# An adjacency kernel of two graph layers: 48 instead of 36 second-layer batches run during the read, and each chunk's work is spread over three slots

## What is computed

```
# layer 0
o  = (adj == 1) @ (x @ w1) + (adj == 2) @ (x @ w2) + (adj == 3) @ (x @ w3) + bias
x1 = layernorm(x + o)
# layer 1: attention over the neighbours
h  = x1 @ W.T + b
e  = leaky_relu(h @ we1 + be1 + (h @ we2 + be2).T, 0.01)
out = layernorm(x1 + softmax(where(adj > 0, e, -9e15), axis=1) @ h)
```

## Time and profile before

| | |
|---|---|
| median of 3 runs | 1693.44 us (1690.89 to 1693.66) |
| the profiled execution | 1693.23 us, its span 1691.6 us |
| TensorE (PE) matmuls busy | 1462.5 us, 86% of the span |
| VectorE (DVE) busy | 1094.2 us, 65% |
| ScalarE (ACT) busy | 959.4 us, 57% |
| GpSimd (POOL) busy | 202.4 us, 12% |
| mean granted TensorE clock | 0.951 of full speed |

### The profile page before, as it was taken

The page is one execution under the profiler, slowest core; times in us unless marked ns, Lnnn a source line. Parts: engine busy times, 40 slices in busy tenths (PEclk is TensorE's granted clock), DMA queues, the critical chain, the costliest instruction groups (busy, mean ns, idle before and its releaser), DMA issues. The chain is left out here.

```text
span 1691.6 us, 19291 instructions
## 1 busy us (share of the span) xinstructions
PE 1462.5 (86%) x6934; PEld 672.6 (40%) x6934; DVE 1094.2 (65%) x2384; ACT 959.4 (57%) x1454; POOL 202.4 (12%) x188
## 2 busy tenths in 40 slices
PE   3687686986998998989979489999999999999996
PEld 1333342442443443444434134444444444444443
DVE  3557666867697676667764766556666666666563
ACT  2233423624355444444633667777787878888774
POOL 1112214122122121120210400000000000000000
PEclk9889899997999998999989689999999999999998
DMA  9999889889888898897890210000011000000100
GB/s 118 122 129 103 97 86 109 97 76 105 87 91 94 79 97 95 77 110 82 84 112 4 62 38 7 25 25 2 26 44 32 25 26 26 26 26 25 32 1 14
DMA packets 122435, 106.45 MB, mean 63 GB/s; under 512 B 4768, under 2 KB 114912, under 8 KB 122336
## 3 DMA queue, kind: packets, MB, share of 16 engines
q0 software_dynamic: 67584, 67.12, 43.9%
q1 hardware_dynamic: 54752, 38.05, 7.9%
HBM read 294.39 MB, written 12.09 MB: 181 GB/s over the span
## 5 line engine op out<-in xcount | busy, mean ns | idle before, releaser
L968 ACT ACTIVATE neg_masks<-e_row,cols 128x512 int8<-128x512 f32 x1024 | 640.7, 708 | 208.4 <-PE ps L1164 149.4
L1164 PE MATMUL ps<-pos_masks,tables 128*128 128x512 fp8e4 x2048 | 622.3, 386 | 63.4 <-DVE pos_masks L597 58.3
L1164 PE MATMUL ps<-neg_masks,tables 128*128 128x512 fp8e4 x2048 | 619.4, 384 | 0.0
L1118 PE MATMUL ps<-edge_masks,tables 128*128 128x512 fp8e4 (+1 forms) x2048 | 479.3, 395 | 49.2 <-DVE edge_masks L576 34.1
L595 DVE TENSOR_TENSOR neg_masks<-pos_masks,neg_masks 128x2048 uint16<-128x2048 uint16 x128 | 161.7, 1263 | 281.9 <-ACT neg_masks L968 280.8
L1118 PEld LDWEIGHTS ps<-edge_masks,tables 128*128 128x128 f16 x2048 | 204.8, 101 | 308.5 <-DVE edge_masks L576 37.8
L1164 PEld LDWEIGHTS ps<-pos_masks,tables 128*128 128x128 f16 x2048 | 196.0, 99 | 319.1 <-issue 107.5
L1164 PEld LDWEIGHTS ps<-neg_masks,tables 128*128 128x128 f16 x2048 | 202.7, 99 | 251.4 <-issue 16.6
L576 DVE TENSOR_SCALAR edge_masks<-edges 128x512 uint16<-128x512 uint16 x512 | 109.2, 286 | 171.4 <-ACT edges L959 171.1
L953 ACT ACTIVATE packed_bf<-packed 128x1024 bf16<-128x1024 uint8 x64 | 67.4, 1053 | 211.3 <-DVE packed L566 211.3
L959 ACT ACTIVATE edges<-ps 128x1024 uint8<-128x1024 bf16 x64 | 65.5, 1023 | 190.2 <-PE ps L1130 190.2
(11 more groups left out here) (116 smaller groups left out, 642.7 us busy)
## 6 DMA issues: line engine op xcount, KB each, us to landing
adj_in<-adj POOLq DMA_DIRECT2D x128, 512.0 KB, 11.9
e_row<-e_scratch SPq DMA_DIRECT2D x30, 256.0 KB, 4.3
edges<-x SPq DMA_DIRECT2D x8, 512.0 KB, 12.6
x_rows<-x SPq DMA_DIRECT2D x8, 512.0 KB, 5.0
x_scratch<-x SPq DMA_DIRECT2D x8, 512.0 KB, 8.0
edge_masks<-x_scratch SPq DMA_DIRECT2D x16, 256.0 KB, 3.2
out<-adj_in SPq DMA_DIRECT2D x16, 256.0 KB, 2.5
part_scratch<-a_c_rows SPq DMA_DIRECT2D x14, 256.0 KB, 5.1
```

Source lines behind the costliest of these rows:

```text
L968: ins = e.activation(GN[:, n:n + GR].bitcast(I8), e1row[:, q % 2, :], ACT.Sign, bias=t2[:, JC * c + j:JC * c + j + 1])
L1118: ins = e.matmul(ps[:, h, :], v_hl[:, i, JC * c + j, :], U0[:, n:n + GR].bitcast(kind), start=c == 0 and j == 0 and i == 0, stop=c == NCH ...
L1164: ins = e.matmul(z_bank(q, k), tab[:, c, 2 * k + i, j, :], mask[:, n:n + GR].bitcast(F8A), start=first and j == 0 and i == 0, stop=final a ...
```

## The change

It alters the plan, the order of work in a slot on all five engines, and which engine does three steps.

- **Plan.** 48 batches have slots during the read: 2, 6, 8, 8, 8, 8, 8 behind the groups 0 to 6. From slot 29 on each slot has one. Halves 0 and 1 are worked on in four segments, 2 to 13 in two. 34 segments instead of 30; 18 of them add a stored partial sum instead of 14. Of the 80 remaining batches, the halves 6 to 13 have four each. They start in slot 69.
- **Layer 0 two slots behind.** `layer0(k-2)` instead of `layer0(k-1)` in slot k. `edge_masks` of the first half comes before `check_and_pack`, that of the second half behind it.
- **The turn ends TensorE's slot**, behind the batch. ScalarE copies the turned bits (`edges_of(k-1)`) in the next slot. Its `gates` are issued one slot ahead, ahead of `convert`, but those of a group's first batch (`fresh`) behind `convert`.
- **The tail** takes other slots: `o_of` in halves through one PSUM bank, `v_of` in halves, `x1_of` in off 3, `e1_turn` in off 3.
- **GpSimd keeps the loads** and a small memset. `x_and_bias` and the e products go to VectorE, `table_products` to ScalarE as 16 instructions of 128x128. `table_products_again` stays on GpSimd, in slots K, K+1, K+2.
- Partial sums are loaded into a buffer of their own.

```diff
-KNOWN_COLS = 3
 START = 5
 
+EARLY = {
+    0: [(0, [0]), (1, [0])],
+    1: [(2, [0, 1]), (0, [1]), (1, [1]), (3, [0, 1])],
+    2: [(4, [0, 1, 2]), (0, [2]), (1, [2]), (5, [0, 1, 2])],
+    3: [(6, [0, 1, 2, 3]), (7, [0, 1, 2, 3])],
+    4: [(8, [0, 1, 2, 3]), (9, [0, 1, 2, 3])],
+    5: [(10, [0, 1, 2, 3]), (11, [0, 1, 2, 3])],
+    6: [(12, [0, 1, 2, 3]), (13, [0, 1, 2, 3])],
...
+    segs, slots, seen = [], [], {}
+    for b, part in EARLY.items():
+        segs += part
+        n = sum(len(c) for _, c in part)
+        slots += [NCH * (b + 1) + START + (i * NCH // n if n >= 6 else i) for i in range(n)]
+        for g, c in part:
+            seen.setdefault(g, set()).update(c)
     for g in range(2 * NS):
-        segs.append((g, list(range(min(g // 2 + 1, KNOWN_COLS) if g < 2 * NS - 2 else 0, NS)), False))
-    first = K + START - 1
-    first = max(first, slots[-1] + 1)
-    n2 = sum(len(c) for _, c, p in segs if not p)
-    slots += [first + i for i in range(n2)]
+        segs.append((g, [c for c in range(NS) if c not in seen.get(g, ())]))
+    early = len(slots)
+    slots += [max(K + START, slots[-1] + 1) + i for i in range(16 * NS - early)]
...
-AGAIN = (K, K + 1, K + 3)
+AGAIN = (K, K + 1, K + 2)
...
+            def part_load(q):
+                if PRIOR[q] is None:
+                    return
+                n = ADDS.index(q)
+                if n >= 2:
+                    e.wait_ge(s_ev, ADDS[n - 2] + 1)
+                e.wait_ge(s_pst, 16 * (PRIOR[q] + 1))
+                e.dma_start(part_in[n % 2], part_dram[SEGS[q][0]]).then_inc(s_pld[n % 2], 16)
...
+            q = 0
             for S in range(NS - 1):
                 tail(S)
-                row_of(2 * S)
-                next_rows(S)
-                if S:
-                    part_store(2 * S - 1)
-                row_of(2 * S + 1)
-                part_store(2 * S)
+                for n in range(len(EARLY[S])):
+                    row_of(q)
+                    if n == 0:
+                        next_rows(S)
+                    if q:
+                        part_store(q - 1)
+                    part_load(q)
+                    q += 1
...
-            for k in range(K + 5):
+            for k in range(K + 6):
+                for n, slot in enumerate(AGAIN):
+                    if k == slot:
+                        table_products_again(n)
                 for h in range(2):
                     if 2 <= k + 2 < K:
                         load(k + 2, h)
                 for S, off in tails(k):
-                    if off == 0:
-                        x_and_bias(S)
-                    if off == 2:
-                        e_products(S)
-                    if off == 4:
+                    if off == 3:
                         ones_column(S)
-                        if S < 4 or S == NS - 1:
-                            table_products(S)
...
                 sl = slice(JC * S, JC * (S + 1))
+                e.wait_ge(s_x1, S + 1)
+                e.wait_ge(s_setc, 1)
+                for n, dst in enumerate((yT8, xg[:, :, :])):
+                    e.tensor_tensor(dst, X1[:, :, :], u_b[:, n, :].unsqueeze(1).broadcast_to([P, RB, D]),
+                                    ALU.mult).then_inc(s_pe, 1)
                 e.wait_ge(s_pe, 2 * S + 1)
...
             for k in range(NSLOT):
+                for S, off in tails(k):
+                    if off == 2:
+                        v_of(S, 0)
+                for m in at(k):
+                    masks(m)
+                    after(m)
+                for S, off in tails(k):
+                    if off == 2:
+                        v_of(S, 1)
                 if 1 <= k <= K:
-                    for h in range(2):
-                        edge_masks(k - 1, h)
+                    edge_masks(k - 1, 0)
                 for S, off in tails(k):
-                    if off == 1:
-                        v_of(S)
                     if off == 2:
-                        rs_of(S)
+                        statistics(S)
+                    if off == 3:
+                        e_sums(S)
+                    if off == 5 and (S < 4 or S == NS - 1):
+                        low(S, yT8, xg[:, :, :])
+                for n, slot in enumerate(AGAIN):
+                    if k == slot + 2:
+                        low(4 + n, xr_b, xr[n])
                 if k < K:
                     check_and_pack(k)
+                if 1 <= k <= K:
+                    edge_masks(k - 1, 1)
                 if k < NCH:
                     split_rest(k)
                 if k == 2:
                     weights_spread()
                 if k == 4:
                     weights_copied()
+                for S, off in tails(k):
+                    if off == 0:
+                        x_and_bias(S)
+                    if off == 2:
+                        rs_of(S)
+                    if off == 5:
+                        rows_sum(S)
                 for m in at(k):
-                    masks(m)
-                    after(m)
-                for S, off in tails(k):
-                    if off == 1:
-                        statistics(S)
-                    if off == 3:
-                        e_sums(S)
-                    if off == 5:
-                        if S < 4 or S == NS - 1:
-                            low(S, yT8, xg[:, :, :])
-                        rows_sum(S)
-                for n, slot in enumerate(AGAIN):
-                    if k == slot + 1:
-                        low(4 + n, xr_b, xr[n])
-                if k == K + 7:
+                    for q in ended(m):
+                        exponents(q)
...
+            def table_products(S):
+                e.wait_ge(s_one, S + 1)
+                e.wait_ge(s_er, S + 1)
+                e.wait_ge(s_bd, 2 * (S + 1))
+                for f, dst in ((bq, yT8), (dq, xg[:, :, :])):
+                    for t in range(RB):
+                        ins = e.activation(dst[:, t, :], X1[:, t, :], ACT.Copy, scale=f[:, JC * S + t:JC * S + t + 1])
+                    ins.then_inc(s_pt, 1)
...
+            def fresh(m):
+
+                return SLOTS[m] == NCH * (BATCH[m][1] // 2 + 1) + START
+
             e.wait_ge(s_const, 1)
             for k in range(NSLOT):
+                if k < NCH:
+                    split_high(k)
+                for S, off in tails(k):
+                    if off == 3:
+                        x1_of(S)
+                if 1 <= k <= K:
+                    edges_of(k - 1)
+                for S, off in tails(k):
+                    if off == 4:
+                        e1_turned(S)
+                        b_d_of(S)
+                    if off == 5 and (S < 4 or S == NS - 1):
+                        high(S, yT8, xg[:, :, :])
+                for n, slot in enumerate(AGAIN):
+                    if k == slot + 2:
+                        e.wait_ge(s_l0, 2 * K)
+                        high(4 + n, xr_b, xr[n])
+                for m in at(k + 1):
+                    if not fresh(m):
+                        gates(m)
                 for S, off in tails(k):
                     if off == 2:
                         sd_of(S)
-                if k < NCH:
-                    split_high(k)
-                for m in at(k):
-                    gates(m)
-                    after(m)
                 if k < K:
                     convert(k)
-                    edges_of(k)
                 if k < NCH:
                     split_low(k)
                 for S, off in tails(k):
-                    if off == 0:
+                    if off == 1:
                         y_of(S)
-                    if off == 2:
-                        x1_of(S)
-                    if off == 4:
-                        e1_turned(S)
-                        b_d_of(S)
-                    if off == 5:
-                        if S < 4 or S == NS - 1:
-                            high(S, yT8, xg[:, :, :])
-                for n, slot in enumerate(AGAIN):
-                    if k == slot + 1:
-                        e.wait_ge(s_l0, 2 * K)
-                        high(4 + n, xr_b, xr[n])
+                    if off == 4 and (S < 4 or S == NS - 1):
+                        table_products(S)
+                for m in at(k + 1):
+                    if fresh(m):
+                        gates(m)
+                    after(m)
...
 
             e.wait_ge(s_ident, 4)
             for k in range(NSLOT):
+                if 2 <= k < K + 2:
+                    layer0(k - 2, 0)
                 for S, off in tails(k):
-                    if off == 1:
-                        o_of(S)
-                if 1 <= k <= K:
-                    for h in range(2):
-                        layer0(k - 1, h)
-                if k < K:
-                    turn(k)
-                if k == 3:
-                    weights()
-                for S, off in tails(k):
-                    if off == 4:
-                        e1_turn(S)
+                    if off == 2:
```

(16 more changed lines are left out.)

140 lines of the change are left out of this document (54 added, 86 removed).

## The result

| | before | changed kernel |
|---|---|---|
| median | 1693.1 us | 1649.9 us (1645.8 to 1657.8) |
| ratio | | 0.976, 95% interval 0.973 to 0.979 |
| profiled execution, its span | 1693.2, 1691.6 us | 1649.3, 1647.6 us |
| layer 0 ends | 928.6 us | 970.2 us |
| mean granted TensorE clock | 0.951 | 0.973 |

What follows compares the result with a forecast made beforehand. Bound: TensorE's work per batch slot, plus some 15 us open per group, mostly gates waiting for a stored and reloaded row. 1693.2 with -14.2 + 9.0 + 4.7 - 14.4 - 82.6 = -97.5 gives 1596 us; range 1562 to 1648.

Steps and rivals of the forecast that it cites:

- Slots 13 to 28: Tails of groups 0 and 1 under the read: 208.6 us instead of 222.8, -14.2 us.
- I allow 3 us: Slots 23 and 25: single-batch segments wait for a partial sum's collection and store and another row's load; 3 us allowed.
- The slots without a batch, at 11.15 us: Slots 13 to 28: each slot without a batch costs the chunk pace, 11.15 us with the DMA engines full.
- Slots 29 to 60, +9.0 us: Every slot has a batch: 465.8 us plus allowances for late hand-overs and single-batch segments, 478.8 against 469.8.
- Slots 61 to the end of layer 0, +4.7: End of the read, layer 0 two slots behind and ending in slot 65: 66.0 us against 61.3.
- the switch, -14.4: Seven batches behind the last layer-0 product, chained over tables from x1 read back: about 74 us instead of 88.0.
- 84 batches at 7.51: After the last layer-0 product: 84 batches left instead of 95, rate unchanged at 7.51 us each, -82.6 us.
- The e1 row: Four-batch segments after the read: lands in 3.7 to 5.4 us, about 7 left; otherwise a few us in eight segments.
- GpSimd counted at nothing: GpSimd gives up tail work; pack instructions take 0.43 us instead of 2.47, but nothing more is counted in the sum.
- rival 2: Group starts: PE's 9.9 us stall moves to late pack or gates; six groups, +44, 1640 us; chance 0.2.
- Rival 3: Read: VectorE delays chunk loads; only the eight slots without a batch pay, +20, 1616 us; chance 0.05.
- Rival 4: Batch slots: gates become part of each slot, 16.8 us; over 44 slots +111, 1707 us; chance 0.08, middle case included.

Runs made afterwards that it cites:

- plan36: The changed kernel with the old plan of 36 batches under the read instead of 48: 1701.7 us, ratio 1.006 to the kernel before.
- tp_pool: The changed kernel with `table_products` on GpSimd again, two products per group instead of 16 ScalarE instructions: 1645.4 us, ratio 0.973.
- row_early: The changed kernel with the next segment's row issued on SyncE ahead of the `x` rows and partial sums: 1642.2 us, ratio 0.970.
- row_tail: The changed kernel with row_early and tail_only together: 1610.2 us, ratio 0.950.
- tail_late: combo_tail5 with the batches of groups 0 and 1 alone one slot later, still 48 batches: 1578.6 us, ratio 0.932.
- ac_early: The changed kernel, after the read only, with exponents ahead of the masks and their exp one slot earlier than the root: 1639.4 us, ratio 0.969.
- combo_tail5: The changed kernel with row_early, tp_pool and ac_early, plus a group's tail put behind the pack: 1592.0 us, ratio 0.940.
- tail_tp_act: combo_tail5 with the table products on ScalarE, as in the change: 1593.0 us, ratio 0.942.
- tail_only: The changed kernel with only a group's tail reordered, behind the pack and conversion: 1647.3 us, ratio 0.974.
- combo_start6: The changed kernel with row_early, tp_pool and ac_early, plus every group's first batch a slot later, no fresh gates: 1625.5 us, ratio 0.961.

## Why the prediction was wrong, step by step

- *What bounds the kernel.* Right. TensorE's work fills a slot with a batch (14.3 or 15.2 us per slot from 38 on), and the batches under the read are the gain: 12 of them are worth about 51 us (plan36 less the changed kernel), while the order alone costs about 10 (plan36 less before).
- *"Slots 13 to 28 ... Group 0's tail: two batch slots and six without, 2 x 14.27 + 6 x 11.15 ... -14.2 us".* **This is the step that failed**: +18.6 us against before, 32.8 above the forecast. "With the changed order a slot should cost the larger of the chunk pace and PE's work" left three waits out.
  - *The first batch of a group, at 14.27 us.* For slots 13 and 21 the sum had nothing over PE's pace; the 2.5 us per group come only from slot 29 on, and the table products on ScalarE are named only for group 3. Measured: 26.2 and 22.3 us, 20 us more. TensorE waited 7.71 us for the table in slot 13 and 4.72 for the masks in slot 21, and about 2 us more went each time into matmuls at a granted clock of 0.50. The trace of before already had 4.45 us of the first. tp_pool halves it (3.78), so about half comes from the table products on ScalarE.
  - *"I allow 3 us" for the segments of one batch, and "`convert` no longer waits for the row".* The second is true for a group's first gates only. For the next segment the gates stand ahead of `convert` on ScalarE, and the row behind two other transfers on SyncE. I named this chain for slots 23 and 25 but mis-sized it: slot 25 alone took 22.1 us, 7.8 over 14.3, and row_early, which takes the row out of it, has 15.2. In slot 13 the same wait was 2.01 us.
  - *The slots without a batch, at 11.15 us.* The sum left out the ring of layer 0, edge masks, pack, conversion and turn, of which the trace of before already had the parts, and it put the tail's 4 to 5 us on VectorE nowhere in it. The circle that I did count for a slot with a batch ("12.2 of the 13.8") did not ask when the edge-mask buffer comes free. In slots 13 to 28 this is 7.2 us, in slots 9 to 12, which the sum did not hold, 11.8 against before. Moving the tail out of the ring brought slots 10 and 11 to 12.1 and 11.5.
- That the row and the tail belong together is shown: with both mended (row_tail) slots 13 to 28 take 225.4 us instead of 241.4 and layer 0 ends at 934.5, against 928 forecast. Of what was left there, 16.8 us over the forecast, 12.55 are the wait for the table in slot 13 and 3.26 that for the masks in slot 21. Both went in tail_late: 211.7 us for a forecast of 208.6.
- *Slots 29 to 60, +9.0 us.* Mis-sized: 15.9. The excess lies in slots 29 to 44 (128.5 and 122.3 for groups of eight, then 117.2 and 117.7), those with single-batch segments and table products. The full-work figure without stalls, 465.8, was right: tail_late takes 465.0. "It fits, narrowly" was right for groups without table products, slots of 14.3 and 15.2.
- *Slots 61 to the end of layer 0, +4.7; the switch, -14.4.* Right: 64.3 us for 66.0, 75.4 for 74. `low` takes 2.3 us there instead of 5.83.
- *84 batches at 7.51.* Mis-sized by 10 us: 7.64 each. "The loop over two batches, which the shorter segments don't touch" left out that exp and root belong to different segments and now meet in one slot. ac_early, which parts them, has 7.45. The e1 row, which I had suspected, was not it: behind the read no gate waited for a row.
- *GpSimd counted at nothing.* Right in size for the table products: given back to it they gain 4.5 us (tp_pool, intervals overlap) or 1.0 (combo_tail5 against tail_tp_act). `x_and_bias` and the e products, which left GpSimd too, were not tested alone. The pack instruction that had taken up to 2.47 us (L560) takes 0.43 in all 64 chunks now (L546), as forecast.
- *The rivals.* The result is nearest to rival 2 (1640 us, chance 0.2): the stall moved instead of going. It did so in groups 0 to 3 only, and of the two reasons that it gave one was right in part: the gates behind the table products, slots 13 and 21. The wait for the table itself was in no rival. The price was put at 7.4 us in each of six groups. Measured it was 4 to 12 us in each of the five slots 13, 21, 25, 29 and 37, plus the slots without a batch. Rival 3 (loads late) did not come, though its sign did ("slots without a batch over 13 us": 14.6 and 17.3); tail_only took slots 10 and 11 to 12.1 and 11.5 by order alone. The loads' issues (L461) over the whole run:

```profile
L461 POOL DMA_DIRECT2D adj_in<-adj x128: 740/802/1064, 1.4 to 920.2; - x128
```

Their median is 802 ns, 748 before; the 128 issues sum to 102.0 us, 98.4 before, on an engine that is busy 7% of the span. Of the issues' 807.8 us of waiting, 806.9 are for the pack. The Trainium skill (SBUF — State Buffer, SBUF: two separate sides) has a VectorE instruction in a two-port mode lock GpSimd out of descriptor writing. With twelve batches more on VectorE the trace shows 28 ns more per issue on the mean, and the loads landed in 11.9 us at the median in both kernels. Rival 4 (slower) was wrong for the whole, but plan36 shows that it had been a matter of the batches: the same order with the old plan is slower by 0.6%.

The range was too narrow because two bounds were not opened. The first batches of the groups 0 and 1 stood at 14.27 us, with no allowance, though their slots had taken 29.4 and 25.2. The slots without a batch stood at one value from one row of the kernel before, which is itself a mean: between slots 9 and 28 of that kernel they took 9.6 to 13.1 us.

## What to carry to other kernels

Where a single buffer is filled and read by two engines, count the ring through it (who frees it, what stands ahead of the next step on each engine in it) even in the slots that look idle; work put ahead of the ring's next step lengthens it in full. When a wait is taken away, ask of each strictly ordered queue which instruction now stands there with an unready input; here taking either of two such waits away gave 8 us at most, taking both gave 40. Give the first use of a freshly made operand its own chain: slot 13 waited 7.7 us for the table, and 12.6 once the table's last step stood behind the pack. And a step moved by a slot is cheap where an empty slot lies next to it: two groups' batches one slot later were worth 13 us, while moving every group's (combo_start6) lost 11.5.

## What was not expected of the hardware

- The same 256 KB row took 4.5 us to land in the changed kernel and 12.3 us in tail_only, issued 0.4 us behind a load of 512 KB in both; its landing time is no constant while chunks are loading.
- A wait of 4.72 us was followed by 3.2 us at a granted clock of 0.50: the price of a stall on TensorE is more than its length. In slot 13 7.71 us of waiting were followed by 3.6 us at 0.50. In tail_late, with fewer such waits, slots 29 to 60 ran at 1.00.
- Exp and root in turn cost ScalarE two table loads of 1.28 us per segment. While they fell into different slots, batches came at 7.5 us on the mean, in the kernel before and in ac_early; with both between the same two gates, two of a segment's four intervals were 8.8 us. The kernel before has four intervals of 8.8 us too, two of them with an exp and four output instructions (L1023) between the gates, so the pair is not the only thing that makes one.
